# Attention by whole batches instead of by query tiles, with the scores taken a second time keys-down, in a cross-attention and expert-routing kernel

## What is computed

```python
q = (layernorm(x) @ Wq + bq)      # 16 heads of width 8
k, v = ctx @ Wk + bk, ctx @ Wv + bv
w = softmax(where(mask, -inf, q k^T / sqrt(8)))
x = x + (w v) @ Wo + bo
logits = layernorm(x) @ router_w + router_b   # 8 experts and an identity
gates = the two largest softmax probabilities of each token
x = x + sum over the two: gate * (gelu(xn @ w1[e]) @ w2[e])   # or gate * xn
```

## Time and profile before

| what | value |
|---|---|
| time, median of 3 runs | 253.57 us (253.42 to 253.72) |
| span of the profiled execution (first to last instruction) | 257.3 us |
| that execution's time by the clock of the runs | not shown; the span stands for it |
| TensorE matmul busy | 191.6 us (74%), 1467 instructions |
| VectorE busy | 156.0 us (61%), 498 |
| ScalarE busy | 102.0 us (40%), 210 |
| GpSimd busy | 102.4 us (40%), 148 |
| first maximum of the first tile starts | 24.97 us |
| last slot known | 147.76 us |
| first expert tile on TensorE | 160.5 us |

### The profile page before, as it was taken

One profiled execution on the slowest core, in us unless ns is written; L12 is line 12 of the kernel. 1 busy time (PEld: TensorE's weight loads), 2 busy tenths in 40 slices (PEclk: granted clock), 3 DMA queues, 4 the chain that ended last, 5 costly groups with the idle time before them and its releaser, 6 DMA issues.

```text
span 257.3 us, 5658 instructions
## 1 busy us (share of the span) xinstructions
PE 191.6 (74%) x1467; PEld 169.9 (66%) x1468; DVE 156.0 (61%) x498; ACT 102.0 (40%) x210; POOL 102.4 (40%) x148
## 2 busy tenths in 40 slices
PE   1747899999986599849783200999999999999500
PEld 0516488778765587739782100899999999999500
DVE  2799968788883678938853650254554554554226
ACT  2411565678654476436653310122322322323100
POOL 8293001002047520782057479044554554554600
PEclk9999999999999589997978555599999999999955
DMA  3535892000001000110001031212222222210069
GB/s 98 159 122 215 263 309 83 4 0 0 4 20 44 9 0 0 37 36 0 0 28 50 21 103 50 61 47 74 59 68 64 71 62 68 62 52 11 3 218 271
DMA packets 20303, 18.30 MB, mean 71 GB/s; under 512 B 3255, under 2 KB 16752, under 8 KB 20287
## 3 DMA queue, kind: packets, MB, share of 16 engines
q1 hardware_dynamic: 16831, 13.98, 18.5%
q0 software_dynamic: 2304, 3.75, 4.7%
q10 hardware_dynamic: 1152, 0.37, 0.6%
HBM read 10.60 MB, written 8.50 MB: 74 GB/s over the span
## 4 chain that ended last, share of the span: by engine, by line
PE 48%; DVE 23%; issue 9%; DMA 6%; ACT 4%; another core or an unknown queue 4%; SPq 3%; POOL 1%; DVEq 0%; POOLq 0%; ACTq 0%
PE ps_s L926 14%; PE ps_av L807 8%; PE ps_av L935 7%; PE ps_o L935 6%; PE ps_t L798 5%; DVE mx L1058 4%; DVE sc L1062 3%; DMA pair_sb<-pairs 2%; PE ps_t L917 2%; DMA ctx_sb<-in_ctx 2%; DVE v_sb L1030 1%; PE ps_s L774 1%; DVE v_sb L1032 1%; SPq L317 1%
## 5 line engine op out<-in xcount | busy, mean ns | idle before, releaser
L523 POOL DMA_INDIRECT pairs<-yg,xg x40 | 39.1, 976 | 44.1 <-issue 22.7
L701 ACT ACTIVATE hT<-ps_s 128x512 f32<-128x512 f32 x40 | 23.9, 597 | 61.5 <-PE ps_s L926 61.5
L480 POOL DMA_INDIRECT slots<-rows,slot x32 | 31.7, 990 | 39.1 <-issue 18.3
L926 PE MATMUL ps_s<-xgT,w_now 128*128 128x128 f32 x320 | 44.4, 283 | 0.0
L807 PEld LDWEIGHTS ps_av<-vbd,exT 128*128 128x128 f32 x320 | 40.9, 205 | 2.4 <-issue 2.4
L807 PE MATMUL ps_av<-vbd,exT 128*128 128x99 f32 (+1 forms) x320 | 41.8, 286 | 0.8 <-issue 0.8
L926 PEld LDWEIGHTS ps_s<-xgT,w_now 128*128 128x128 f32 x320 | 40.5, 199 | 0.1
L1215 DVE COPY w_now<-w_sb 128x512 f32 x40 | 17.2, 429 | 21.5 <-issue 16.9
L798 PE MATMUL ps_t<-ident,ex 128*128 128x128 f32 x160 | 28.1, 314 | 0.1
L547 ACT COPY exT<-ps_t 128x384 f32<-128x384 f32 (+1 forms) x48 | 24.1, 514 | 7.5 <-PE ps_t L798 4.2
L1058 DVE TENSOR_REDUCE mx<-ps_s 128x8 f32<-128x616 f32 x32 | 25.4, 793 | 2.5 <-PE ps_s L774 1.9
(11 more groups left out here) (157 smaller groups left out, 239.9 us busy)
## 6 DMA issues: line engine op xcount, KB each, us to landing
xg<-slots SPq DMA_DIRECT2D x40, 65.0 KB
pairs<-zeros SPq DMA_DIRECT2D x4, 512.0 KB, 4.0
w_sb<-in_L_ffn_w SPq DMA_DIRECT2D x1, 2048.0 KB, 9.7
pair_sb<-pairs SPq DMA_DIRECT2D x3, 512.0 KB, 4.7
x_sb<-in_x SPq DMA_DIRECT2D x4, 256.0 KB, 6.7
out<-out_sb SPq DMA_DIRECT2D x3, 256.0 KB, 2.9
pairs<-yg,xg POOLq DMA_INDIRECT x40
slots<-rows,slot POOLq DMA_INDIRECT x32
```

Source lines behind the costliest of these rows:

```text
L480: pool.indirect_dma_start(slots, bass.IndirectOffsetOnAxis(ap=slot[k][:, t, c:c + 1], axis=0), rows[:, t, :], None, bounds_check=ROWS - 1, ...
L523: pool.indirect_dma_start(pairs, bass.IndirectOffsetOnAxis(ap=xg[:, u, D + 1:D + 2].bitcast(U32), axis=0), yg[:, u % 4, :], None, bounds_c ...
L701: act.activation(hT[:, u % 2, :], ps_h[u % 2], ACT.Gelu).then_inc(h_used, 1)
L926: m = pe.matmul(ps_h[par][:, P * c:P * (c + 1)], w1_now[:, par, P * c:P * (c + 1)], xgT[:, par, :], start=True, stop=True)
```

## The change

The loop and the tile order go; attention works on a whole batch of 512 queries, written out for four batches.

- The scores are taken twice. `scores` is as before, a half of a tile at a time into one pair of banks (`ps_b`), but only for the maxima: VectorE's `maxima` writes them into `mz`, and four transposes (`transpose_max`) and a copy turn a batch's maxima into `mT`.
- `scores_t` takes the scores again with the keys on the partitions and all 512 queries as columns: in each of three rounds r (128 of the 384 padded key rows of a group), four matmuls on four row strips, then four more on the same strips and banks that add `minus` times `mT`, which subtracts each head's maximum. ScalarE's `exponentials` writes the result straight into `exT`, so there are no transposes and no copies of the exponentials.
- `sums` and `weigh` multiply `exT` by a matrix of ones (masked) and by the values. Each uses, in each round, four matmuls of 32 columns, whose results lie on four different strips of 32 PSUM partitions of one bank, 512 queries wide.
- The reciprocal of the sums is Exp(-Ln(s)) on ScalarE and one Newton step on VectorE (`seed_sums`, `refine_sums`); `normalise` multiplies the values. The result already has the features on partitions, so no transpose stands ahead of the projection (`project_out`).
- While batch n is exponentiated, TensorE scores batch n+1, projects queries of n+2 and finishes batch n-1. The last batch's closing work is done in two segments of two tiles each (before: three tiles and one).
- Two banks (`ps_r`) are used in turn by an order written out in a list.
- Masked keys of all four batches have buffers of their own: VectorE builds the first, POOL the other three before it does anything else. POOL no longer fills `vbd` with zeros. `padrows`, which the load of the expert weights waits for on SP's queue, is written after the first batch's maxima.
- x plus the output bias goes straight into `base_sb`. The buffers of the final addition share memory with `exT`. The expert stage's code is the same, with other PSUM tensors of the same size.

```diff
-            def less_max(kind, n, t):
-                i = n * TT + t
-                par = t % 2
-                for half in range(2):
-                    dve.wait_ge(s_full, i * 2 + half + 1)
-                    s = ps_s[:, 2 * half:2 * half + 2, 0:GK].rearrange("p g (h k) -> p g h k", k=NK)
-                    m = mx[:, par, 8 * half:8 * half + 8]
-                    link(dve.tensor_reduce(m, s, AX.X, ALU.max))
-                    if half == 0 and (kind != "first" or t >= 2):
-                        dve.wait_ge(ex_ready, i - 1)
-                    o = sc[:, par, 2 * GK * half:2 * GK * (half + 1)]
-                    dve.tensor_tensor(o.rearrange("p (g h k) -> p g h k", g=2, k=NK), s,
-                                      m.rearrange("p (g h) -> p g h", g=2).unsqueeze(3)
-                                      .to_broadcast([P, 2, HG, NK]), ALU.subtract).then_inc(s_used, 1)
...
-            def attend(kind, n, t, i, b, par, project_before=True, last_tile=False):
-                def transposes(p):
-                    number, bank = fill(kind, n, FILLS[f"T{t}"] + p)
-                    begin_fill(number)
-                    a, z = PIECES[p]
-                    for c in range(a, z):
-                        m = pe.transpose(ps_t[bank][:, P * (c - a):P * (c - a + 1)], ex[:, par, P * c:P * (c + 1)],
-                                         ident[:, :])
-                    m.then_inc(t_full, 1)
-                def products(p):
-                    number, _ = fill(kind, n, FILLS[f"T{t}"] + p)
-                    pe.wait_ge(t_used, number + 1)
-                    for c in range(*PIECES[p]):
-                        v = vflat[:, bass.ds((b * NCH + c) * VC, VC)]
-                        m = pe.matmul(ps_av[:, (DH + 1) * head0[c]:(DH + 1) * head0[c] + VC],
-                                      exT[:, par, P * c:P * (c + 1)], v, start=c == 0, stop=c == NCH - 1,
-                                      skip_group_check=True)
-                    return m
...
+            def scores(n, t, h):
+                k = (n * TT + t) * 2 + h
+                if k > 0:
+                    pe.wait_ge(b_used, k)
+                for g in (2 * h, 2 * h + 1):
+                    i = pe.matmul(ps_b[:, g - 2 * h, 0:GK], qT[n % 2][rows_of(g), P * t:P * (t + 1)],
+                                  kbd[n][rows_of(g), 0:GK], start=True, stop=True)
+                i.then_inc(b_full, 1)
+            def transpose_max(n):
+                ps = fill_begins(pe, ("MT", n))
+                pe.wait_ge(max_ready, n + 1)
+                for t in range(TT):
+                    i = pe.transpose(ps[:, P * t:P * (t + 1)], mz[:, t, :], ident[:, :])
+                fill_ends(i, ("MT", n))
+            def scores_t(n, r):
+                k = (n * NC + r) * 2
+                if r == 0:
+                    bank, at = PLACE[("MT", n)]
+                    pe.wait_ge(r_used[bank], at + 1)
+                if k > 0:
+                    pe.wait_ge(a_used, k)
+                c = slice(P * r, P * (r + 1))
+                for g in range(G):
+                    pe.matmul(ps_a[:, g, :], kbd[n][rows_of(g), c], qT[n % 2][rows_of(g), :], start=True, stop=False)
+                for g in range(G):
+                    i = pe.matmul(ps_a[:, g, :], minus[rows_of(g), c], mT[rows_of(g), :], start=False, stop=True)
+                    if g % 2 == 1:
+                        i.then_inc(a_full, 1)
+            def sums(n, rs):
+                for r in rs:
+                    if r == 0:
+                        fill_begins(pe, ("S", n))
+                    pe.wait_ge(a_used, (n * NC + r) * 2 + 2)
+                    for g in range(G):
+                        i = pe.matmul(ps_r[PLACE[("S", n)][0]][rows_of(g), :], onesbd[:, r, n, :],
+                                      exT[n % 2][:, r, g, :], start=r == 0, stop=r == NC - 1, skip_group_check=True)
+                if rs[-1] == NC - 1:
+                    fill_ends(i, ("S", n))
+            def weigh(s, rs):
+                n, w = SEGS[s][0] // TT, width(s)
+                for r in rs:
+                    if r == 0:
+                        fill_begins(pe, ("AV", s))
+                    for g in range(G):
+                        i = pe.matmul(ps_r[PLACE[("AV", s)][0]][rows_of(g), 0:w], vbd[:, r, n, g, :],
+                                      exT[n % 2][:, r, g, cols(s)], start=r == 0, stop=r == NC - 1,
+                                      skip_group_check=True)
+                if rs[-1] == NC - 1:
+                    fill_ends(i, ("AV", s))
...
+            for n in range(B):
+                ahead, behind = n + 1 < B, n >= 1
+                scores_t(n, 0)
+                if ahead:
+                    bank, k = PLACE[("Q", n + 1)]
+                    pe.wait_ge(r_used[bank], k + 1)
+                    pe.wait_ge(kbd_more, n + 1)
+                    scores(n + 1, 0, 0)
+                if behind:
+                    weigh(n - 1, [0, 1])
+                if ahead:
+                    scores(n + 1, 0, 1)
+                if behind:
+                    weigh(n - 1, [2])
+                if n >= 2:
+                    ranks(n - 2)
+                scores_t(n, 1)
+                if ahead:
+                    scores(n + 1, 1, 0)
+                if behind:
+                    project_out(n - 1)
+                if n + 2 < B:
+                    transpose_xn(n + 2)
+                if ahead:
+                    scores(n + 1, 1, 1)
+                scores_t(n, 2)
+                if ahead:
+                    scores(n + 1, 2, 0)
+                if n + 2 < B:
+                    project_q(n + 2)
+                if ahead:
+                    scores(n + 1, 2, 1)
+                if behind:
+                    transpose_x2n(n - 1)
+                if ahead:
+                    scores(n + 1, 3, 0)
+                if not ahead:
                     logits(n - 1)
+                sums(n, [0])
+                if ahead:
+                    scores(n + 1, 3, 1)
+                sums(n, [1, 2])
+                if behind and ahead:
+                    logits(n - 1)
+                if ahead:
+                    transpose_max(n + 1)
+            weigh(L0, range(NC))
+            weigh(L1, range(NC))
+            ranks(B - 2)
...
+            def exponentials(n, r):
+                for h in range(2):
+                    act.wait_ge(a_full, (n * NC + r) * 2 + h + 1)
+                    act.activation(exT[n % 2][:, r, 2 * h:2 * h + 2, :], ps_a[:, 2 * h:2 * h + 2, :],
+                                   ACT.Exp).then_inc(a_used, 1)
+            def seed_sums(n):
+                ps = fill_arrives(act, ("S", n))
+                if n > 0:
+                    act.wait_ge(u_ready, n)
+                act_own.link(act.activation(y0[:, :], ps[:, :], ACT.Ln))
+                act.activation(y0[:, :], y0[:, :], ACT.Exp, scale=-1.0).then_inc(y0_ready, 1)
...
+            for n in range(B):
+                exponentials(n, 0)
+                if n + 2 < B:
+                    store_xn(n + 2)
+                if n >= 2:
+                    router_exp(n - 2)
+                    store_ranks(n - 2)
+                exponentials(n, 1)
+                if n + 2 < B:
+                    store_xnT(n + 2)
+                if n >= 1:
                     seeds2(n - 1)
+                exponentials(n, 2)
+                if n + 2 < B:
+                    store_q(n + 2)
+                if n >= 1:
                     norm2(n - 1)
+                    store_x2nT(n - 1)
+                if n + 1 == B:
+                    store_logits(n - 1)
+                    seed_sums(n)
+                else:
+                    seed_sums(n)
+                    if n >= 1:
+                        store_logits(n - 1)
+                    store_mT(n + 1)
+            router_exp(B - 2)
+            store_ranks(B - 2)
+            seeds2(L0)
+            norm2(L0)
...
+            def maxima(n, t, h):
+                k = (n * TT + t) * 2 + h
+                dve.wait_ge(b_full, k + 1)
+                if n > 0 and t == 0 and h == 0:
+                    bank, at = PLACE[("MT", n - 1)]
+                    dve.wait_ge(r_full[bank], at + 1)
+                to = mz[:, t, :].rearrange("p (g r) -> p g r", g=G)[:, 2 * h:2 * h + 2, 0:HG]
+                i = dve.tensor_reduce(to, ps_b[:, :, 0:GK].rearrange("p g (h k) -> p g h k", k=NK), AX.X, ALU.max)
+                i.then_inc(b_used, 1)
...
+            def refine_sums(n):
+                dve.wait_ge(y0_ready, n + 1)
+                i = dve.tensor_tensor(ssum[:, :], ps_r[PLACE[("S", n)][0]][:, :], y0[:, :], ALU.mult)
+                fill_is_read(i, ("S", n))
+                bank, k = PLACE[("S", n)]
+                dve.wait_ge(r_used[bank], k + 1)
+                dve.scalar_tensor_tensor(uinv[:, :], ssum[:, :], 2.0, y0[:, :], ALU.subtract,
+                                         ALU.mult).then_inc(u_ready, 1)
+            def normalise(s):
```

(31 more changed lines are left out.)

1037 lines of the change are left out of this document (435 added, 602 removed).

## The result

The changed kernel takes **283.76 us** (282.53 to 285.28, 4 runs) against 253.64 (253.42 to 254.47) of the kernel before beside it: ratio 1.1174, 95% interval 1.1129 to 1.122. I had forecast 255.3, with a range of 247 to 271. Slower was right; the size was not, and the time lies outside the range.

The account below looks back on a forecast made before the run. Attention was taken as bound by TensorE's queue. Stages 34.4 + 20.2 + 24.9 + 25.6 + 13.6 + 30.8 put the last slot at 149.5 against 147.8, so 253.57 + 1.7 = 255.3 us; range 247 to 271.

Parts of the forecast that it names:

- The base: Whole kernel: sum made against the profiled span of 257.3 us, its difference carried unchanged to the 253.57 us median.
- The two loop idles: Second loop round and loop exit: unexplained TensorE idles of 5.39 and 4.01 us go with the loop, 9.4 in all.
- the rival of idles that stay: Unrolling does not remove the idles: one piece is +2.4, the loop's two +9.4, giving 257.7 to 264.7 us; chance 0.08.
- Opening: Start to first exponentials' scores: 34.4 us against 25.0 before, with eight maxima and scores alternating at 1.65 each, 13.2.
- Batches: Batches 1 and 2: 24.9 and 25.6 us, including waits of 2.9 (1.6 for `norm2`) and 4.9 (partly before maxima).
- The low clock: TensorE, less busy from 20 to 54, stays slow to 35 or through batch 0: 260.8 to 264.2 us; chance 0.10.
- Column tiles: `sums` and `weigh` on TensorE: four column tiles run at once, 0.89 us per round.
- The rival of slower tiles: Column tiles in `sums` and `weigh` run less than fourfold: 261.9, 279 or 331 us; chance 0.12.
- Changes of shape: TensorE in the batches: each change of tile shape costs 0.2 us, bounds 0 and 0.3; 11, 15 and 14 changes.
- the free rival: Changes of tile shape on TensorE cost nothing: last slot at 144.1, 249.9 us, faster; chance 0.30.
- Closing: From the last exponential to the last slot, with `norm2`, logits, `sums` and two router passes: 30.8 us.
- POOL's sends: After the closing's slots: sends and identity work end at about 157, 5 us before the experts start at 162.1.

Follow-up runs that it names:

- before_again: The kernel before the change, with no edit, run again for a profile that comes with its own time: 251.32 us.
- x2_late: Changed kernel, batches 1 and 2: second norm's transposes moved behind the sums, logits behind the transposes of the maxima; 279.08 us, 1.116 of the kernel before.
- reordered: Changed kernel, whole computation in another order (opening with two bank pairs, values weighed behind sums, closing rearranged, identity part later); 249.71 us, 0.988 of the kernel before.
- identity_last: Changed kernel with POOL's weighting of batch 2's identity part moved behind the last batch's sends; 280.42 us, 1.118 of the kernel before.
- close_b: Changed kernel with the last batch's sums and weighted values taken round by round, ahead of batch 2's norm transposes and logits; 279.33 us, 1.122 of the kernel before.

## Why the prediction was wrong

Three steps failed above all: rows on TensorE behind a new wait were priced at the fast pace, the other work in the opening's queue was put at nothing, and the base was taken from an unusually long execution. The miss is 28.5 us: 19.7 in the stages up to the last slot, 1.4 from there to the experts (14.0 against 12.6), 0.7 behind (97.6 against 96.9), 5.5 from the execution that I took as the base (257.3 against 251.8), and 1.2 because the profiled execution lies under the median.

- **The base.** "I make the sum against the span and carry the difference over unchanged": failed. That execution was some 5.5 us longer than the ones timed, and its last slot 6.1 later than in before_again. Against 141.6 my own sum, 149.5, is a loss of 7.9 and about 261.5 us, inside the range (before_again is itself 2.3 us under the median, so this is the most that the base accounts for).
- **The two loop idles**, 9.4 us: not there in before_again, and in the execution read the first covered a wait for the norm. The changed kernel has none either, so the rival of idles that stay fell too; there was nothing of this size to gain.
- **Opening**, 34.4 forecast, 43.2 measured: 8.8 over. The order and the alternation were right, three terms were not. First, 2.1 is VectorE: the maxima began at 22.11, not 20.0, behind three operations beside POOL that I had priced by size and that took 1.11, 1.23 and 1.18. The Trainium skill (SBUF — State Buffer, Who interferes with whom) says that VectorE and GpSimd lock one pair of ports against each other. The trace agrees (1.2 us here, 0.16 without POOL), and the earlier trace rows may have shown it already with 3.72 us for one copy; no run has that copy without POOL beside it. Second, 4.7: between the first five maxima TensorE's queue also holds a spread of the values, the transposes and the projection of batch 1 (2.08, 1.11 and 2.08); the sum let maxima and halves alternate with nothing between them, without a reason, and the first four cycles took 11.3 instead of 6.6. Third, 1.1: the last four, with nothing between, took 7.7, 2.30 a cycle (1.40 + 0.90) where 1.65 had taken the pace of a late row; my own row of the slow pace stood for these operations. The remaining 0.9 is transposing and copying the maxima.
- **Batches.** At the fast pace the sum was good: x2_late's batch 1 is 25.4 and those of reordered, with less waiting at the end, 23.2 and 22.7, against 24.9 and 25.6. The steps that failed are "1.6 for `norm2`" and the waits at the maxima, costed at their own length: the rows behind them run at 1.40, 1.94 and 3.64, and batches 1 and 2 were 4.4 and 3.3 over.
- **The low clock** stood among the rivals with 0.10 and at most 264.2 us, because I let it last through batch 0 only and never asked which new waits would bring it back. That is the step that cost most: most of the 4.4 and 3.3 in batches 1 and 2, 3.5 in the closing and a part of the opening. Which waits bring it back, and which do not, stays open.
- **Column tiles** ran fourfold: two rounds of weighted values, 16 matmuls, start 1.85 apart (66.78 to 68.63), 0.93 a round against 0.89. The rival of slower tiles fell, and with it the estimate of 1.3 times that the prediction worked out from the Trainium skill (TensorE: Matmul & The Clock Gate, Part 3, Measured speedup vs the span model).
- **Changes of shape** cost something: a half between column tiles holds TensorE for 0.72 (68.63 to 69.35) and one that comes behind `scores_t`, of its own shape, for 0.62 (66.16 to 66.78), 0.19 and 0.09 over the streaming of 0.535; the two rounds between them take 0.07 over theirs. That is about 0.13 a change as an estimate, between the 0.2 taken and the free rival. It lies below the 0.15 at which the prediction let the sign turn: its own sums, 146.1 at 0.1 and 149.5 at 0.2, give about 147.1, ahead of the 147.8 it set out from. With the measured price its own terms and base would have given "faster"; that "slower" came out is owed to the slow pace and the opening, and was luck as far as this term goes.
- **Last batch**, 12.9 against 13.6: right.
- **Closing**, 33.8 against 30.8: the steps were right, transposes, logits and `sums` ran at 1.09, 1.94 and 5.18 instead of 0.7, 1.1 and 2.9, together 3.5. (The forecast's own terms add up to 30.5, not 30.8; nothing hangs on it.)
- **POOL's sends** "stay under the pads": failed. They end last and start the experts; identity_last and close_b moved that start, to 12.6 and 16.1 us behind the last slot, so that the last slot was not the one number to ask for. In before_again, too, sends are on the chain with 9% of the span.
